# A decoder layer on one core: the cross product from one float32 product to three rounded ones, with GpSimd splitting the context

## The reference

```python
x = _layernorm(x + attn(x))        # 16 heads of 64, causal
x = _layernorm(x + xattn(x, ctx))  # key j allowed for query i where j % 128 == i
x = _layernorm(x + ffn(x))         # 8 experts, the best 2 of each token, and a shared one
```

## Time and profile before

| | |
|---|---|
| median of 3 runs | 487.77 us (486.56 to 488.73) |
| the profiled execution | 485.99 us |
| its span, first to last instruction | 484.2 us |
| TensorE busy | 455.3 us, 94% |
| weight loads (overlap TensorE) | 398.2 us, 82% |
| VectorE, ScalarE, GpSimd busy | 305.2, 288.2, 202.3 us |
| mean granted TensorE clock | 0.988 |

### The profile page before, as it was taken

One profiled execution on the slowest core, in us unless ns is written; L12 is line 12 of the kernel. 1 busy time (PEld: TensorE's weight loads), 2 busy tenths in 40 slices (PEclk: granted clock), 3 DMA queues, 4 the chain that ended last, 5 costly groups with the idle time before them and its releaser, 6 DMA issues.

```text
span 484.2 us, 11184 instructions
## 1 busy us (share of the span) xinstructions
PE 455.3 (94%) x3613; PEld 398.2 (82%) x3613; DVE 305.2 (63%) x1253; ACT 288.2 (60%) x911; POOL 202.3 (42%) x248
## 2 busy tenths in 40 slices
PE   6999999999999999999999999988998999999971
PEld 6887888988888888898888887878887889999951
DVE  4286696757665665696655769586977334333576
ACT  2677555675565765567656565773544545765563
POOL 2997395400002002111044443534424777777720
PEclk9999999999999999999999999999989999999987
DMA  7831121410100000010021213110122443333755
GB/s 245 267 122 45 59 89 45 138 38 1 35 12 0 2 12 34 24 66 1 1 67 27 96 65 100 45 57 34 44 78 70 162 143 121 114 121 119 250 208 173
DMA packets 26542, 40.33 MB, mean 83 GB/s; under 512 B 3199, under 2 KB 17555, under 8 KB 26483
## 3 DMA queue, kind: packets, MB, share of 16 engines
q1 hardware_dynamic: 21532, 27.88, 18.9%
q0 software_dynamic: 3408, 9.34, 5.1%
q10 hardware_dynamic: 1547, 2.40, 1.5%
HBM read 26.98 MB, written 12.63 MB: 82 GB/s over the span
## 4 chain that ended last, share of the span: by engine, by line
PE 72%; ACT 10%; DVE 9%; DMA 4%; issue 2%; SPq 1%; POOL 1%; ACTq 0%; DVEq 0%; POOLq 0%
PE bank L294 16%; PE bank L296 14%; PE bank L295 14%; PE bank L806 5%; PE bank L768 5%; ACT probs L1107 4%; PE bank L779 4%; PE bank L831 3%; DMA ex_raw<-y_dram 2%; PE bank L946 2%; DVE ot_lo L1359 1%; PE bank L936 1%; PE bank L854 1%; DMA xacc<-in_x_t 1%; PE bank L960 1%
## 5 line engine op out<-in xcount | busy, mean ns | idle before, releaser
L1107 ACT ACTIVATE probs<-probs,negmax 128x128 f32<-128x128 f32 x256 | 99.6, 393 | 49.9 <-DVE negmax L1334 49.9
L294 PE MATMUL bank<-w_hi,ot_hi 128*128 (+1 forms) x284 | 83.2, 293 | 3.7 <-ACT qkv L1078 3.6
L295 PE MATMUL bank<-w_lo,ot_hi 128*128 (+1 forms) x284 | 80.5, 283 | 0.0
L296 PE MATMUL bank<-w_hi,ot_lo 128*128 (+1 forms) x284 | 80.2, 282 | 0.0
L573 POOL DMA_INDIRECT xg_dram<-xacc,place x32 | 31.6, 988 | 101.0 <-PE bank L779 41.1
L1334 DVE CUSTOM_DVE_ANT_0 probs<-bank,mask 128x128 f32<-128x128 f32 x256 | 61.2, 284 | 15.3 <-PE bank L768 15.3
L294 PE MATMUL bank<-xt_hi,w_hi 128*128 128x512 f32 x144 | 61.1, 424 | 2.5 <-DVE xt_lo L1305 1.5
L294 PEld LDWEIGHTS bank<-w_hi,ot_hi 128*128 128x128 f32 x284 | 54.2, 191 | 7.5 <-ACT qkv L1078 5.5
L1070 ACT ACTIVATE qkv<-bank,cols 128x512 f32<-128x512 f32 x64 | 42.1, 679 | 29.3 <-PE bank L296 29.3
L296 PE MATMUL bank<-xt_hi,w_lo 128*128 128x512 f32 x144 | 56.9, 395 | 0.0
L295 PE MATMUL bank<-xt_lo,w_hi 128*128 128x512 f32 x144 | 56.9, 395 | 0.0
(11 more groups left out here) (220 smaller groups left out, 1052.5 us busy)
## 6 DMA issues: line engine op xcount, KB each, us to landing
qkv<-xg_dram SPq DMA_DIRECT2D x39, 129.0 KB
ex_raw<-in_w_experts SPq DMA_DIRECT2D x18, 256.0 KB
w_raw<-in_w_quads SPq DMA_DIRECT2D x10, 256.0 KB, 7.0
xacc<-in_x SPq DMA_DIRECT2D x4, 512.0 KB, 3.8
ex_raw<-in_w_cross SPq DMA_DIRECT2D x4, 512.0 KB, 3.3
w_raw<-in_ctx_t_in ACTq DMA_DIRECT2D x4, 512.0 KB
w_raw<-in_w_quads SPq DMA_DIRECT2D x3, 512.0 KB, 6.8
xacc<-in_x_t SPq DMA_DIRECT2D x3, 512.0 KB, 7.2
```

Source lines behind the costliest of these rows:

```text
L294: pe.matmul(o, a_hi, b_hi, start=first, stop=False)
L295: pe.matmul(o, a_hi, b_lo, start=False, stop=False)
L296: return pe.matmul(o, a_lo, b_hi, start=False, stop=last)
L1107: nc.scalar.activation(tile, tile, ACT.Exp, scale=-1.0, bias=negmax[:, s.par, h, j:j + 1], accum_out=sums[:, s.par, h, j:j + 1]).then_inc( ...
```

## The change

The cross product uses `three` on rounded operands. ScalarE's copy becomes `wvo_hi`, and VectorE adds `wvo_lo` in slot 8. GpSimd splits each group's context into the place of that group's transposed input, `xt_hi` and `xt_lo`, which is free by then; TensorE waits for the split in place of the transfer. The other edits make room in SBUF: half of the broadcast row bias is no longer loaded, `upto` becomes bf16, `ranked` is computed in the place of `hot`, and `tile_base` moves into an old staging tile.

```diff
-        wvo = sb("wvo", [P, KT, D])
+        wvo_hi = sb("wvo_hi", [P, KT, D], F32R)
+        wvo_lo = sb("wvo_lo", [P, KT, D], F32R)
-        bcast = sb("bcast", [P, 2 * D])
+        bcast = sb("bcast", [P, D])
-        upto = sb("upto", [P, 2 * NE, 2 * NE])
+        upto = sb("upto", [P, 2 * NE, 2 * NE], BF16)
-        ranked = sb("ranked", [P, 2, GT, NE])
-        tile_base = sb("tile_base", [P, TILES])
+        tile_base = late[:, 3 * D + TILES:3 * D + 2 * TILES]
...
+            def split_ctx(g):
+
+                pool.wait_ge(in_ctx, 16 * (g + 1))
+                pool.wait_ge(proj_v, 2 * QUADS * (g + 1))
+                here = slices(g, GROUP)
+                split(xt_hi[:, :, here], xt_lo[:, :, here], ctx_t, ctx_split)
...
             number_rows()
+            split_ctx(0)
             split_expert(0)
             split_expert(1)
             x2_lo(0)
+            split_ctx(1)
             for r in range(GT):
                 send_in_slot(0, r)
             x2_lo(1)
             for i in range(2, 5):
                 split_expert(i)
+            split_ctx(2)
             for r in range(GT):
                 send_in_slot(1, r)
...
             x2_lo(2)
+            split_ctx(G - 1)
             split_expert(14)
             split_expert(15)
             send(2, 0)
...
             def cross(g, half):
                 if half == 0:
-                    pe.wait_ge(in_ctx, g * 16 + 16)
+                    pe.wait_ge(ctx_split, g + 1)
                     if g == 0:
-                        pe.wait_ge(wvo_ready, 1)
+                        pe.wait_ge(wvo_lo_ready, 1)
...
                     for k in range(KT):
-                        mm = pe.matmul(o, ctx_t[:, k, slices(2 * half + j, P)], wvo[:, k, :],
-                                       start=False, stop=(k == KT - 1))
+                        tok = slices(g * GT + 2 * half + j, P)
+                        mm = three(pe, o, xt_hi[:, k, tok], xt_lo[:, k, tok], wvo_hi[:, k, :], wvo_lo[:, k, :],
+                                   False, k == KT - 1)
...
-            act.dma_start(bcast[:, :], row_bias.partition_broadcast(P)).then_inc(in_bcast, 16)
+            act.dma_start(bcast[:, :], row_bias[0:D].partition_broadcast(P)).then_inc(in_bcast, 16)
...
-                nc.scalar.activation(wvo[:, :, :], bank[7][:, :].rearrange("p (k n) -> p k n", k=KT), ACT.Copy
+                nc.scalar.activation(wvo_hi[:, :, :], bank[7][:, :].rearrange("p (k n) -> p k n", k=KT), ACT.Copy
...
+            def wvo_low():
+                dve.wait_ge(wvo_ready, 1)
+                nc.vector.tensor_tensor(wvo_lo[:, :, :], bank[7][:, :].rearrange("p (k n) -> p k n", k=KT),
+                                        wvo_hi[:, :, :].bitcast(F32), ALU.subtract).then_inc(wvo_lo_ready, 1)
...
-            inside, small = {}, {}
+            inside, small = {SPG: [wvo_low]}, {}
```

More of the change, by code:

```diff
@@ L245, in decoder_program @@
         in_gate = sem("in_gate")
-        wvo_step, wvo_ready = sem("wvo_step"), sem("wvo_ready")
+        wvo_step, wvo_ready, wvo_lo_ready = sem("wvo_step"), sem("wvo_ready"), sem("wvo_lo_ready")
+        ctx_split = sem("ctx_split")
         w_split = [sem("w_split_qk"), sem("w_split_v"), sem("w_split_o")]
@@ L1496, in places @@
                 for i in range(2):
-                    last = nc.vector.tensor_tensor(ranked[:, i, :, :], hot[:, i, :, :], ranks, ALU.mult)
+                    last = nc.vector.tensor_tensor(hot[:, i, :, :], hot[:, i, :, :], ranks, ALU.mult)
                 at = issue(last)
@@ L1500, in places @@
                 dve.wait_ge(dve_step, at)
-                at = issue(nc.vector.tensor_reduce(place_f[:, :, :], ranked[:, :, :, :], AX.X, ALU.add))
+                at = issue(nc.vector.tensor_reduce(place_f[:, :, :], hot[:, :, :, :], AX.X, ALU.add))
                 yield
```

## The result

| | before | after |
|---|---|---|
| median | 487.17 us (486.56 to 488.73, 4 runs) | 480.75 us (480.38 to 480.89, 4 runs) |
| the profiled execution | 485.99 us | 480.87 us |
| its span | 484.2 us | 479.1 us |
| mean granted TensorE clock | 0.988 | 0.991 |

The ratio is 0.9856 (95% interval 0.9835 to 0.9877): 6.4 us faster by the medians, where 2.3 were forecast. The time lies outside the range given.

A forecast was written before the change was run, and what follows sets the result against it. The prediction took TensorE, with the float32 cross product on its path, to bound the kernel. TensorE's -2.3 us and 0 for all else took the median from 487.77 to 485.5 us, range 483.8 to 488.0.

The forecast's parts named there:

- TensorE's term: Cross product: rounded matmuls 0.12 us apart save 0.29 us in each of eight halves, 2.3 us in all.
- rival D: Cross product: the two more weight loads a tile show, giving 487.8 us, or 491.6 in full; chance 0.04.
- ScalarE, VectorE, room: The rounded copy, wvo_low hidden in slot 8, and the edits that make room: 0, with 0.3 us either way.
- GpSimd: Context split, 3.9 us four times (cast 1.51, subtraction 2.36), done before TensorE's cross product wants it: 0.
- The port: GpSimd's subtractions hold VectorE through the shared SBUF port: hidden in slot 8, up to 1.3 us in slot 30, taken as 0.
- the Sum: Whole kernel: TensorE's 2.3 us less and 0 for all else, so the median falls from 487.77 to 485.5 us.
- Rival C: First expert tiles, 360 to 365 us: TensorE comes earlier and keeps its clock, about 1 us more gained, 484.5; chance 0.11.
- B: Slots behind the halves, or slot 30: part of the gain is given back, 486.3 to 487.3 us; chance 0.19.
- E: GpSimd's four subtractions hold VectorE on the path: slower, up to 495.0 us; chance 0.06.

The follow-up runs named there:

- e2: The changed kernel run again with no edit: 479.56 us, ratio 0.9838 to the kernel before.
- e4: The changed kernel with the cross product again one float32 product, on the unsplit context and wvo_hi, low part left out: 487.03 us, 0.9984 to the kernel before.
- e3: The kernel before with only the edits that make room in SBUF: 487.55 us, ratio 1.0002.
- e7: The changed kernel with 32 small matmuls (64 instructions) added behind all of TensorE's work: 481.06 us, 0.9844 to the kernel before.
- e11: The changed kernel with 14 identity matmuls filling TensorE's idle time ahead of the last sums: 480.66 us, 0.9850 to the kernel before.
- e5: The kernel before with 32 small matmuls (64 instructions) added behind all of TensorE's work: 484.93 us, ratio 0.9934.
- e12: The kernel before with 128 small matmuls (256 instructions) added behind all of TensorE's work: 484.61 us, ratio 0.9936.
- e17: The kernel before with 192 small matmuls (384 instructions) added behind all of TensorE's work: 485.35 us, one run.
- e18: The kernel before with 320 small matmuls (640 instructions) added behind all of TensorE's work: 485.91 us, one run.
- e1: The kernel before run again with no edit: 487.96 us, ratio 1.0003.
- e10: The kernel before with 8 identity matmuls ahead of the first projection, where TensorE stands idle: 486.72 us, ratio 0.9973.
- e15: The kernel before with 64 one-column activations behind all of ScalarE's work; only the head was read: first real product at 9.53 us.
- e6: The kernel before with 64 one-column memsets behind all of GpSimd's work: 487.77 us, ratio 0.9998.
- e9: The kernel before with 8 small matmuls (16 instructions) added behind all of TensorE's work: 488.00 us, ratio 1.0002.
- e14: The kernel before with 16 small matmuls (32 instructions) added behind all of TensorE's work: 488.98 us, one run.
- e16: The kernel before with 64 one-column memsets behind all of VectorE's work; only the head was read: first real product at 9.70 us.
- e8: The changed kernel with 19 identity matmuls ahead of the first projection, to delay its expert stage: 484.90 us, 0.9929 to the kernel before.
- e13: The changed kernel with one float32 cross product, low part left out, and 32 small matmuls behind TensorE's work: 485.38 us, 0.9954 to the kernel before.

## Why the prediction was wrong

**TensorE's term: right.** 0.12 us steps, 1.68 us a half, 0.305 us saved in each of the six halves between slots 8 and 30 (221.10 to 219.27), so 2.4 us for eight. The loads stay hidden, and rival D is out: e2 and e4, which differ in just these products, take 219.29 and 221.12 us from slot 8 to slot 30. The Trainium skill (TensorE: Matmul & The Clock Gate, "The mechanism") has loads overlap only between different row groups, but the same section also lets a load to the background weight buffer be pulled ahead of running matmuls; the 0.12 us steps here, with a load of 0.19 us for each matmul, are in line with the second and not with the first.

**ScalarE, VectorE, room: right.** e3 is nothing. `wvo_low` took 0.68 us at 98.83, hidden.

**GpSimd: right, its terms a little high.** A cast is 1.04 us (1.51 assumed), a subtraction 2.39 to 2.71 (2.36), all at least 14 us early.

**The port: right in its place, small in its price.** The normalisation was stretched to 1.56 and 1.60 us in slot 8 with no wait of TensorE behind it. In slot 30 the price was 0.5 us (slot 30 to 31: 4.71 us before, 5.21 after), not 1.3; e4, with the old products and the new splits, has it too (5.20). Up to the expert stage all of the kernel's own terms come to 2.1 us: its first tile starts at 352.23 to 352.98 in the changed kernel, e2, e7 and e11, and at 354.50 to 354.83 in e5, e12, e17 and e18, whose heads are as early (slot 0 at 16.05 to 16.74 and 16.13 to 16.60). From slot 8 on it is 2.4 us: 259.28 us to the first expert tile in e2, 261.69 in e4.

**The failing step is the Sum**, "-2.3 + 0 = -2.3 us". It took the rest of the program as unchanged because no edit touches it. What the runs showed in its place is two more gains:

- *The first transfers, about 3 us, shown by edits.* With 64 instructions more, TensorE's stream is fetched in 32 packets in place of 31, the first transposed input lands sooner, and TensorE's first real product starts 1.2 to 2.7 us sooner. That brings slot 0 from 18.1 us (before, e1, e4, e10, e15) to 16.4. And five of the nine late heads without e10's filler (e3, e6, e9, e14, e16) lost the clock too, slot 0 at 20.06 to 21.02; none of the ten early ones did. The mean of those nine is 19.4 us, so 3 us against 16.4; e5 and e12 measured 3.5 and 2.9 us by their medians. Why the transfers depend on the length of TensorE's stream stays open.
- *Behind the head, 1.5 to 1.8 us more than the kernel's own 2.1 to 2.4, not settled.* e7 is 3.9 us under e5 and e11 3.9 under e12, pairs with equal heads (3.87 and 3.95). Part of the rest is the clock. Its mean over the three-product executions (the changed kernel, e2, e7, e11) is 0.991 (0.989 in e8), over the padded one-product ones (e5, e12, e13) 0.987. Among executions of one and the same kernel (129 of 14 kernels) a granted clock higher by 0.001 goes with 0.29 us less, so 0.004 is worth some 1.2 us (an estimate). One fall costs 0.94 us at the first expert tiles and some 1.7 us in the last sums. But the clock isn't all: executions that list 0.990 or 0.991 take 480.4 us in the three-product kernels (12 of them) and 484.1 in the padded ones (8), 3.7 us apart. In traces without a fall among the expert tiles the way from the first of them to the last sums is 106.53 and 106.75 us in the changed kernel and e2, 107.22 to 107.62 in e5, e17 and e18 (but 107.29 in e11), which no experiment explains. Rival C was right in kind and in size (1 us), given too little chance (0.11), and its reason, that TensorE comes earlier to the first expert tiles, isn't borne out: e7 comes as early and has the fall there. Falls were seen in both kinds, with and without idle time ahead. Why three products make them rarer stays open.

Together the head's 3.0 and the 3.9 us of the pairs are 6.9 us, where the changed kernel measured 6.4 (first result) and 8.1 (e2).

**Rivals B and E** did not come. The 0.5 us given back in slot 30 was mostly recovered: from slot 31 to the first expert tile it is 35.84 us before and 34.80 after, 1.04 less, of which the two halves of group 3 are 0.6. e4, which keeps the old halves, gets the other 0.5 back as well (35.37).

## What to carry to other kernels

A change that only shortens work in the middle can still move the first 10 us: compare the landing of the first transfers and the packets of the instruction queue before the gain is put down to the edit. A sum over the edited lines is a forecast for them alone; the control that separates the two is a version with the old work and the new number of instructions. Idle time of TensorE ahead of its first products can cost more than itself when the clock falls there, and the few matmuls of the identity that filled part of it in e10 were cheap.

## What the runs showed of the hardware

- The rate of the first transfers depends on the length of TensorE's program: 144 to 164 GB/s from 2 to 4 us in the ten traces with 31 instruction packets, 231 to 273 in the ten with more. The threshold lies between 32 and 64 instructions over this kernel's. No instruction packet runs in those first microseconds in the four traces read for it (before, after, e5, e12; the first lies between 12 and 20 us), so no instruction packet competes with the transfers there; where program and inputs lie in memory would fit, but no run tested it.
- 128 matmuls of 8 bf16 columns took 3.34 us at the end of e12, 26 ns each.
- The clock fell in traces to its lower level (0.50) for some 3.4 us, in places for 6.8 (e3 and e16 in the head), also with TensorE busy and idle for no more than 0.30 us at once in the 14 us ahead of it (e1, 346 to 360 us), and in one of two traces of near-identical timing (e7, but not e2).
- A 128x4 cast of VectorE took 0.69 us in place of 0.17 while GpSimd's subtraction ran (315.53 in the changed kernel's trace).
